# Loading the projection's token blocks two steps ahead, from slots 11 and 13, and summing the batch mean in another PSUM bank

## The reference

```
xn  = layernorm(x)                                   # 64 tiles of 128 tokens
# branch 1: linear attention, causal, 16 heads of 32
q, k, v = elu(xn @ wq) + 1, elu(xn @ wk) + 1, xn @ wv
S_kv += k v^T ; z += k ; o = q S_kv / (q z)          # scanned over the tokens
# branch 2: softmax attention, 16 heads of 32, not causal
q, k, v = xn @ Wq.T + bq, xn @ Wk.T + bk, xn @ Wv.T + bv
h = softmax(scale * (q / |q| + e) k^T) v
out = x + o @ wo + (h * gates(h)) @ Wp.T + bp
```

## Time and profile before

| | |
|---|---|
| time of three runs | 3792.5, 3795.33 (the median), 3801.5 us |
| time of the profiled execution | 3798.58 us |
| its span, first to last instruction | 3796.8 us |
| lying around the span | 1.8 us |
| granted clock of TensorE, mean | 0.988 of full |

### The profile page before, as it was taken

How to read it: one execution, slowest core, us unless ns; L and a number is a source line. 1 busy time by engine, 2 the same in 40 slices (tenths; PEclk the granted TensorE clock), 3 DMA queues, 4 the chain that set the end, 5 groups by cost and what they waited for, 6 DMA issues and landing times.

```text
span 3796.8 us, 146980 instructions
## 1 busy us (share of the span) xinstructions
PE 3668.4 (97%) x65560; PEld 1717.7 (45%) x65560; DVE 3353.0 (88%) x3512; ACT 2704.8 (71%) x2681; POOL 653.9 (17%) x277
## 2 busy tenths in 40 slices
PE   5899999999999999999999999999999999999999
PEld 3644444444444444444444444444444444444333
DVE  8589999999999999988999989998888888988996
ACT  4477777777777777777777777776777777777663
POOL 4111111111121221121121211221011010010121
PEclk8899999999999999999999999999999999999999
DMA  6522334232332333342442432433231231322233
GB/s 223 148 60 67 63 69 86 65 75 51 100 85 80 91 94 93 69 112 64 96 101 65 110 85 74 99 90 76 70 93 54 84 87 48 98 71 63 79 94 105
DMA packets 414319, 326.27 MB, mean 86 GB/s; under 512 B 210328, under 2 KB 362360, under 8 KB 413044
## 3 DMA queue, kind: packets, MB, share of 16 engines
q1 hardware_dynamic: 412964, 308.43, 31.8%
q10 hardware_dynamic: 720, 8.39, 0.5%
HBM read 228.64 MB, written 75.48 MB: 80 GB/s over the span
## 4 chain that ended last, share of the span: by engine, by line
PE 84%; ACT 5%; issue 4%; DVE 4%; DMA 2%; SPq 0%; DVEq 0%; ACTq 0%; POOL 0%; POOLq 0%
PE ps L1160 32%; PE ps L1343 23%; PE ps L1329 19%; ACT prob L985 4%; PE ps L1244 3%; PE ps L1273 2%; DVE acc L1899 2%; PE ps L1207 2%; PE ps L1267 1%; PE ps L1289 1%; DMA et<-in_qe 1%; PE ps L1310 0%; PE ps L1253 0%; ACT r L929 0%; DVE zc L1845 0%
## 5 line engine op out<-in xcount | busy, mean ns | idle before, releaser
L985 ACT ACTIVATE prob<-ps 128x2048 f32<-128x2048 f32 x1024 | 1925.2, 1880 | 654.2 <-PE ps L1329 652.4
L1899 DVE TENSOR_TENSOR acc<-acc,prob 128x2048 f32<-128x2048 f32 x896 | 2073.8, 2314 | 30.7 <-ACT prob L985 10.0
L1343 PE MATMUL ps<-prob,v 128*32 128x512 f32 x8192 | 1093.3, 605 | 0.7 <-issue 0.7
L1329 PE MATMUL ps<-q_hi,k_hi 32*128 32x512 f16 x4096 | 419.9, 385 | 32.7 <-ACT prob L985 25.7
L1160 PE MATMUL ps<-x_hi,w_hi 128*32 128x512 f16 x4096 | 442.8, 385 | 8.2 <-DVE xbar L1699 4.6
L1160 PE MATMUL ps<-x_lo,w_hi 128*32 128x512 f16 x4096 | 442.1, 384 | 0.0
L1160 PE MATMUL ps<-x_hi,w_lo 128*32 128x512 f16 x4096 | 441.4, 384 | 0.0
L1329 PE MATMUL ps<-q_lo,k_hi 32*128 32x512 f16 x4096 | 410.1, 375 | 1.8 <-issue 1.8
L1329 PE MATMUL ps<-q_hi,k_lo 32*128 32x512 f16 x4096 | 410.6, 375 | 1.3 <-issue 1.3
L793 POOL TENSOR_TENSOR rn<-ss,minus_half 128x16 f32<-128x16 f32 x64 | 232.7, 3636 | 830.1 <-ACT ss L887 830.1
L1343 PEld LDWEIGHTS ps<-prob,v 128*32 128x32 f32 x8192 | 161.5, 108 | 435.4 <-issue 435.4
(11 more groups left out here) (270 smaller groups left out, 4446.1 us busy)
## 6 DMA issues: line engine op xcount, KB each, us to landing
x_hi<-xhi_scratch SPq DMA_DIRECT2D x62, 512.0 KB, 6.4
x_lo<-xlo_scratch SPq DMA_DIRECT2D x62, 512.0 KB, 7.7
x_in<-in_x SPq DMA_DIRECT2D x64, 256.0 KB, 7.2
rq<-rq_scratch SPq DMA_DIRECT2D x64, 256.0 KB
rdl<-rdl_scratch SPq DMA_DIRECT2D x64, 256.0 KB
y<-in_x SPq DMA_DIRECT2D x64, 256.0 KB, 6.1
out<-y SPq DMA_DIRECT2D x64, 256.0 KB, 6.0
rden<-rden_scratch SPq DMA_DIRECT2D x63, 256.0 KB
```

Source lines behind the costliest of these rows:

```text
L985: s_.activation(prob[i % 3][:], ps[:, 0:HG, :], ACT.Exp, bias=-SHIFT, scale=inv_c[:, g:g + 1] if wide else 1.0 / CQK).then_inc(exped, 2)
L1329: last = t_.matmul(bank[h], kk[rows32(h), cols128(kt)], qq[rows32(h), :], start=(kk is kh and qq is qh), stop=(kk is kl and not wide))
L1343: last = t_.matmul(bank[OUT][rows32(h), :], v[m // NB % 2][:, kt, rows32(h)], prob[i % 3][:, h, :], start=(kt == 0), stop=(kt == TT - 1))
L1899: v_.tensor_tensor(acc[:], acc[:], prob[i % 3][:], ALU.add).then_inc(summed, 1)
```

## The change

There are two parts.

1. `load_block` is called for block n + 2 in place of n + 1, and in two pieces: x_hi at SP's slot 11, x_lo at slot 13. `load_x` moves from slot 3 to slot 13, behind x_lo. Both halves wait for `ql_proj` to reach n + 1: the buffer is the one that block n's projections read, and LQ_'s are the last.
2. `mean_x` writes columns 256 to 259 of bank X1 and stands in slot 8 + lag, ahead of the small transpose, and PE no longer waits for `xbar_ready` before LK_. It waits for it before `turn_phk`, which overwrites the bank. DVE's copy moves one slot later and waits for `bound_turned` too.

```diff
@@ SP
-            def load_block(n):
+            def load_block(n, parts):
                 first = (n // (NB * NG) * NB + n % NB) * BT
                 for i in range(2):
                     sp.wait_ge(xt_stored[i], (first + BT) // 2 * 32)
                 sp.wait_ge(ql_proj, n - 1)
-                for tile, src in ((x_hi, xhi_d), (x_lo, xlo_d)):
-                    sp.dma_start(tile[n % 2][:].rearrange("p t k n -> p t (k n)"),
-                                 src[first:first + BT].rearrange("t p e -> p t e")).then_inc(xb_loaded[n % 2], 16)
+                tile, src = parts
+                sp.dma_start(tile[n % 2][:].rearrange("p t k n -> p t (k n)"),
+                             src[first:first + BT].rearrange("t p e -> p t e")).then_inc(xb_loaded[n % 2], 16)
@@ SP, kt == 3
-                        if n is not None and 2 <= n + 1 < NBLK:
-                            load_block(n + 1)
                         if o is not None and f is None:
                             load_use("h", o)
-                        if t is not None and t + 1 < NT:
-                            load_x(t + 1)
@@ SP, kt == 11 and after
+                        if n is not None and n + 2 < NBLK:
+                            load_block(n + 2, (x_hi, xhi_d))
                     if kt == 12 and mp is not None:
                         store_h_hi(mp)
+                    if kt == 13:
+                        if n is not None and n + 2 < NBLK:
+                            load_block(n + 2, (x_lo, xlo_d))
+                        if t is not None and t + 1 < NT:
+                            load_x(t + 1)
@@ PE, mean_x
-                    last = t_.matmul(X0[:, k:k + 1], xsum[:, cols128(k)], ones_s[:], start=True, stop=True)
+                    last = t_.matmul(X1[:, XM + k:XM + k + 1], xsum[:, cols128(k)], ones_s[:], start=True, stop=True)
@@ PE, kt == 7 + lag
-                        if t is not None and t % TT == TT - 1:
-                            mean_x(t // TT)
-                            pe.wait_ge(xbar_ready, t // TT + 1)
@@ PE, kt == 8 + lag, n % NB == NB - 1, ahead of the transpose of kmx1
+                            if t is not None and t % TT == TT - 1:
+                                mean_x(t // TT)
@@ PE, kt == 11 + lag, ahead of turn_phk
+                            if t is not None and t % TT == TT - 1:
+                                pe.wait_ge(xbar_ready, t // TT + 1)
@@ DVE
-                    if kt == 7 + lag and t is not None and t % TT == TT - 1:
+                    if kt == 8 + lag and t is not None and t % TT == TT - 1:
+                        dve.wait_ge(bound_turned, n // NB + 1)
                         keep_mean(t // TT)
```

More of the change, by code:

```diff
@@ L433, in build @@
         POOL_CONST = 13
+        XM = 2 * P
         SPLITS, SPLITS_WOP = (3, 4, 6, 9, 12, 14), (3, 6, 9, 12)
@@ L1698, in keep_mean @@
                 dve.wait_ge(mean_done, b * NG)
-                v_.tensor_copy(xbar[:].rearrange("p k o -> p (k o)"), X0[:, 0:KC]).then_inc(xbar_ready, 1)
+                v_.tensor_copy(xbar[:].rearrange("p k o -> p (k o)"), X1[:, XM:XM + KC]).then_inc(xbar_ready, 1)
             def shift_k(g):
```

## The result

The changed kernel takes 3771.84 us (median of 6 runs, 3770.49 to 3775.99), the one before 3798.07 in the same rounds (6 runs, 3792.5 to 3801.5). The ratio is 0.9933 with an interval of 0.9923 to 0.9944: faster by 0.7%, some 26 us. Its profiled execution took 3772.89 us with a span of 3771.1, against 3798.58 and 3796.8 before.

What follows compares the result with a forecast made beforehand. PE was taken to bound the kernel (84% of the chain), with gains only where it stands still. Batch mean -6.9, attention steps -15.4 and start -4.0 sum to -26.3 us from 3798.58, giving 3772, range 3762 to 3790.

Steps and rivals of the forecast that it cites:

- Case 1: Whole kernel: gains in batch mean, attention steps and start all come, 3772 us, own range 3764 to 3781; chance 0.60.
- Late fetches behind a burst: Attention slots 4 to 7: PE's instructions arrive late behind slot 3's loads; 10.5 us idle, 19.5 us lost in 20 slots.
- Rival 2: Attention steps: fetches stay late from PE's density, or move to slots 13 and 15; only the mean gains, 3788 us; chance 0.20.
- Attention steps, -15.4: Slots 4 to 7: moving the loads wins 85% of 19.5 us, 16.6, less 1.2 taken back; bounds -19.5 to 0.
- The give-back at slot 13: Steps 19, 47 and 55: PE's stop had let DVE catch up, so slot 13 takes back 1.2 us.
- Batch mean, -6.9: Steps 11, 27, 43: removing PE's wait saves 9.8 us, less 2.1 for products and 0.8 for DVE; bounds -9 to -4.5.
- the term for DVE: Mean's copy: DVE stands 0.5 us for `bound_turned`, PE later waits for y; half of 0.8 each charged, 0.8 in all.
- Start, -4.0: Before the first exponential: two late fetches go, -6.4 us, plus 0.9 and 1.5 lost; bounds -6.4 and +2.
- the two prices: Before the first exponential: x_in landing late costs 0.9 us, the last weights' store to DRAM 1.5 us.
- Rival 3: Steps with a mean: the wait for `bound_turned` and lost catch-up cost their upper bound, start gives nothing; 3778 us; chance 0.10.
- rival 5: Attention steps: fewer losses at slot 4 and new ones at slot 13, 3782 us; chance 0.06.
- Rival 4: Slots 12 to 15: bursts from slot 11 starve PE in nearly every step, 59 us against 26 won, 3825 us; chance 0.04.

Runs made afterwards that it cites:

- the copies in slot 3: Changed kernel plus two 512 KB DRAM-to-DRAM copies that nobody reads, in rows of 1 KB, issued in SP's slot 3 of each step with a block: 3787.2 us.
- those in slot 13: Changed kernel plus two unread 512 KB DRAM-to-DRAM copies issued in SP's slot 13, behind x_lo: 3771.6 us.
- the kernel with nothing in slot 3: Changed kernel with the output tile's store and the y and h loads moved from slot 3 to slot 8: 3788.4 us; 3763.2 with bias on 8 columns.
- the run with the token tile in slot 3: Changed kernel, but in the steps before 0 the token tile is asked for in slot 3 again: 3771.3 us.
- four copies in slot 13: Changed kernel plus four unread 512 KB DRAM-to-DRAM copies in slot 13 of each step with a block: 3771.3 us.
- the short and the long bias addition: Changed kernel with slot 3's store and loads in slot 8; GpSimd adds y's bias to 8 columns (3763.2 us) or all 512 (3788.4 us).

## Why the prediction was right, and where not

Predicted 3772, measured 3771.8. Case 1 of the list, the main forecast, is what happened, and both mechanisms are shown. That the number fits to 0.2 us is luck: the mean's part brought 1.4 us more than its term, the start 2.2 less, and the sum hangs on the base too. It was taken from the profiled execution, 3798.58; from the 3795.33 of the three runs that stood ahead of the prediction the same terms give 3769. The terms one by one:

- **Late fetches behind a burst** (the reading on which most rests): shown, by the copies in slot 3 against those in slot 13 and by the packets of instructions. The 10.5 us in 17 waits leave out two waits of other lines, 2.0 us, which were late fetches too. Rival 2 is out as far as time goes. PE's density alone is not enough: the waits went with the bytes while the instructions stayed. And the waits did not move with the burst: none at the border of a block came back in slots 12 to 15, at 1, 2 or 3 MB there. The lateness did move with it, as rival 2 had it, by 0.8 to 1.5 us on the mean, but PE had the slack. The Trainium skill, "Runtime: NRT & Kernel Launch", Instruction fetch mechanics, has the crossing from one block to the next mostly hidden; the kernel with nothing in slot 3 agrees with it at 0.0 us of issue waits, the kernel with 1.8 MB there disagrees at 17.2. "DMA: Bandwidth & Descriptors", Queues, rings and completion order, has an engine take turns packet by packet, which would keep a fetch from waiting for a burst; 2.00 us in the middle of a group of products speak against it as the whole story. The packets of instructions start late and then take their usual 1 us, so whatever holds them lies ahead of their start; what it is, no run shows.
- **Attention steps, -15.4**: measured -15.8. The share of 85% was a choice, and nothing in the trace fixed it; it happened to fit. Slots 4 to 7 (without the two of the mean) are 21.2 us shorter in the kernel with nothing in slot 3 than in the one before, and 15.9 shorter in the changed one: 75% of a bigger sum, where I had 85% of 19.5. The give-back at slot 13 in steps 19, 47 and 55 was put at 1.2 and was 0.5, in step 19 alone.
- **Batch mean, -6.9**: -8.3 by the exponentials' starts, 9 us by the run with the mean alone. Removed in slot 7 was 4.96 + 4.55, within a hundredth what I read. In step 11 slot 8 gives 1.42 back and slots 9 and 10 take 0.98, where I had put 0.3. Off in size is the term for DVE: the wait for `bound_turned` came to 0.23 us in place of 0.5, and slot 13 took back 0.1 us in each of steps 27 and 43, where I had charged 0.4. The products cost 0.7 and 0.6 us in slot 8, and not 1.05, plus 0.3 in slot 9 in step 27; slot 8 of step 27 lasts 4.04 us, where I had said near 4.4.
- **Start, -4.0**: mis-sized, -1.8 in the pair of traces, with the first exponential at 198.3 and not 196. The two fetches are on time and the clock stays at 1.00, as said, but neither of the two prices that I put against that shows in a run. For x_in late (0.9) the run with the token tile in slot 3 shows no gain beyond the spread of the traces. What took the place of the 2.67 us in step -3 is, in part, a wait that I had not named: PE for DVE's maximum of the keys, 1.49 us at 116.18, which DVE reaches late because the division of o stands ahead of it. Before, this releaser had 1.3 us in one wait in the same stretch, and it has 5.5 us in three now. Its size varies: nine traces with the changed kernel's start put 137.3 to 140.1 us (mean 138.5) between that set-up stage and the first exponential, the kernel before 140.8 and the one with the mean alone 141.6. Against the mean of these two the gain is 2.7 us, so part of "-1.8" was chance. How much the weights' store costs (it lands in 6.2 us in place of 5.4) stays open.
- **Rival 3** (mean's gain handed to DVE) and **rival 5** (new losses at slot 13): hardly a sign. PE's wait for y there grew from 5.0 to 5.6 us in all.
- **Rival 4** (slower): out, by a wide margin. I had put the point of decision at 0.45 us a step, 26 us in all; three times the block's bytes from slot 11 on cost under 3 us.

The wait that was not named, in PE's waits of the first 198 us of the changed kernel:
```profile
PE ps L1283 <- DVE kmx L1826: 5.5, 3, 2.6
```

## What to carry to other kernels

When a long unrolled program shows PE waits with no releaser in the middle of a group of equal products, look for a large transfer issued 5 to 9 us earlier, and move its bytes to a stretch where PE issues fewer instructions: the same bytes cost 15 us at 240 products in 10 us and nothing at 156. Count the instructions, too: here the waits lay a multiple of 256 instructions apart, and that told them from all other waits. A transfer that another engine works on when it lands moves that engine's work too: before moving it, look at what runs beside that work, and whether there is slack behind. And a place in a queue's program is not a place in time: read in the timeline where the issue falls, since a queue with nothing to wait for runs ahead.

## What the runs showed of the hardware

- A stream of instructions of 8.5 MB over 3.8 ms, 1.0% of the DMA engines' time by the page, stops PE by up to 2.7 us at a time when a burst of 1 to 2 MB stands beside it in PE's densest stretch, by 0.1 to 1.1 us now and then with 768 KB, and never in an attention step with 256 KB or less there. All of these waits but one stand at the border of a block of 256 instructions.
- 322 GB/s with a DMA share of 1.01 over 10 us (four copies in slot 13) delayed no exponential and no small transfer by enough to show in the time, though fetches of instructions started 1.5 us later there on the mean. Here is the stretch, from the windows of that kernel:
```profile
1476.00:1486.00 10.00, 9.21 (x159) 4.14 (x161) 9.93 (x10) 6.78 (x8) 0.00 (x0) 1.00 1.01 322
```
- GpSimd's and DVE's two-input additions in SBUF slow each other: DVE's of 128x2048 3.19 us in place of 2.28, its split of 128x512 1.76 in place of 0.68, GpSimd's own 3.32 in slot 7 against 1.28 in slot 11. The Trainium skill, "SBUF — State Buffer", SBUF: two separate sides, says that a DVE operation with two SBUF inputs and a GpSimd operation that reads SBUF lock each other out of a shared port pair. The rows agree, and the 25 us between the short and the long bias addition are what it was worth here.
